# Weighted sums of an attention kernel: one TensorE run of four key blocks per four heads in place of two runs of two

## The chip, the cores and the metric

The kernel runs on one core of a Trainium2 chip. The metric is the device time of one execution in microseconds (us). The kernel before took 989.45 us, the median of 3 runs (988.32 to 992.9).

## What is computed

The reference is one adapter and one transformer block over `x` of 8 sequences, 512 tokens and 256 channels. What matters here is the attention, with 16 heads of 16 channels and a bias and a mask for each pair of tokens:

```
q, k, v = (x @ Wq + bq), (x @ Wk + bk), (x @ Wv + bv)          # split into 16 heads of 16
scores  = einsum('bhqd,bhkd->bhqk', q / sqrt(16), k) + attention_bias
scores  = where(src_mask, -inf, scores)
probs   = softmax(scores, axis=-1)
ctx     = einsum('bhqk,bhkd->bhqd', probs, v)                   # the weighted sums
x       = x + (ctx @ Wo + bo)
out     = x + gelu2(layernorm(x) @ W1 + b1) @ W2 + b2
```

Ahead of it stands an adapter (`gelu(x @ down) @ expert @ up`, residual, layer norm), and a second layer norm whose scale and shift come from a time step.

## The kernel before

**Tiling.** The 4096 rows are cut into 16 chunks of 256 queries (two chunks to a sequence). An iteration `i` of the main loop holds the attention of chunk `i`; the loop runs over `i` = 0 to 16, the last one only finishes. The norm and projections of chunks `i+1` and `i+2`, the output projection of chunk `i-1` and the feed-forward part of chunks `i-1` and `i-2` are spread over the same iteration.

**Slots.** An iteration has 32 slots, `t` = 0 to 31. A slot is one tile of scores: 128 queries of one head against all 512 keys. Such a tile goes through the engines in this way:

- SyncE loads the bias of a head (two tiles) into one of 8 buffers `bias_s`, once PE has turned the head that used the buffer before.
- POOL subtracts the mask (L490, once for a head).
- PE computes the scores, `score(t)` (L806), into one of two banks `sc`. It waits until DVE has finished tile `t-2`, by semaphore `smax`.
- DVE adds bias and takes the row maximum, `find_max(t)` (L1338), a custom instruction and a short read of its accumulator `mx` behind it, which counts `smax`.
- ACT takes the exponential, `soften(t)` (L952).
- Four slots later (`LAG`) PE transposes the tile, `turn(n)` with `n = t-4` (L813), four blocks of 128 by 128, into one of two banks `tp`. It waits for the exponential and until tile `n-2` has been moved out of the bank.
- ACT, or DVE for the tiles 8, 10, 11, 13, 15, 17, 20, 23, 24, 25 and 27 of an iteration, copies it into the buffer `pT`, `move(n)` (L958, L1345). On ACT, the move of a slot stands ahead of the exponential of that slot.

**The weighted sums.** Four heads (8 tiles) make a group `g`; `pT` has a buffer for each of two groups. When the 8 tiles of a group have been moved, PE multiplies them with the values, `weigh` (L772): for each of four key blocks `kt`, four matmuls, one per head, each of 128 by 32 weights. Their `tile_position` puts them side by side in the array's columns, and each writes 32 partitions of the bank `pv`. Two groups accumulate into one `pv`, which DVE then multiplies with the inverse sums (L1318).

**What sets the order.** Each engine runs its program in order. Where the extra work of an iteration stands is written by hand in tables such as `PE_AT`: the whole part is the slot; fraction .0 is ahead of the slot's score, .3 between its score and its turn, .6 behind its turn. The engines never look ahead: PE's order alone decides when a score and a turn are issued. In `PE_AT` before, a group's sum has two entries, so the run stands in two halves, one ahead of the score of slot 14 and one ahead of the score of slot 15 for the first group, 22 and 23 for the second, 30 and 31 for the third; the fourth stands in the next iteration, ahead of 6 and 7. This text calls them place 14, place 22, place 30 and place 6. The last group of all stands in iteration 16, where no score or turn is left between its two halves.

Of the kernel before, what the change touches and what calls it, by code (L numbers as in the profile page):

```python
# [25 lines left out]
NG = H // GH  # L26
TI = 2 * H
TG = 2 * GH
KT = S // P
# [13 lines left out]


PE_AT = dict(up=0.3, v=(1.0, 2.0), q=(8.6, 10.0), xt1=12.6, k=(15.6, 16.3), down=(24.3, 25.3),
             pv=((14.0, 15.0), (22.0, 23.0), (30.0, 31.0), (6.0, 7.0)), spread=(23.3, 7.3))
ACT_AT = dict(q=(11.0, 12.3), widen=(18.3, 2.3), spread=(24.6, 8.0), k=(17.0, 18.0), xT1=14.0, gelu=26.6)
DVE_AT = dict(x1=1.6, st0=2.3, mv0=2.6, v=3.0, n1=4.0, n2=6.3, st1=7.0, mv1=7.6, m1=8.3, m2=10.6, q=(11.6, 13.0),
              k=(17.6, 18.6), recip=(17.6, 1.6), ctx=(25.3, 9.3))
# [58 lines left out]
def wait(eng, sem, value):  # L108

    if value <= 0:  # L110
        return
    eng.wait_ge(sem, value)
# [7 lines left out]
def on_act(n):  # L120

    return n % TI not in DVE_MOVES


def moved(n, by_act):

    return sum(on_act(k) == by_act for k in range(n % TI)) + n // TI * (21 if by_act else 11)


def head_of(hh):  # L130

    return 8 * (hh // 8) + 2 * (hh % GH) + hh // GH % 2
# [17 lines left out]
def build(nc, x, x_t, t_tok, e_tok, bias, mask, downT, upT, up_b, experts, gamma, beta,  # L150
# [16 lines left out]
    with ExitStack() as ctx:  # L167
# [3 lines left out]
        def ps(name):  # L171
            return ctx.enter_context(nc.psum_tensor(name, [P, 512], F32))

        def sem(name):
            return ctx.enter_context(nc.semaphore(name))
# [86 lines left out]
        pv = ps("pv")  # L262
# [42 lines left out]
        s = {n: sem(n) for n in names}  # L305
# [246 lines left out]
        def _(pe):  # L552
# [63 lines left out]
            def fold_expert(b, bank, j):  # L616
                return pe.matmul(bank[0:A + 1, j * D:(j + 1) * D], ew_t[:, b, :], up_w, start=True, stop=True)
# [42 lines left out]
            for b in range(6, 8):  # L660
                last = fold_expert(b, tp[0], b % 2)
# [8 lines left out]
            def body(i, attn, prev, nxt, pre, qv, down):  # L670
                a, c = i + 2, i + 1
                AT = PE_AT

                def norm_steps(t):
                    if pre and t == AT["up"]:
                        wait(pe, s["a_xt1"], a)
                        wait(pe, s["d_out"], i - 2)
                        adapter_up(a)
                    if qv and t in AT["q"]:
                        if t == AT["q"][0]:  # L680
                            pe.wait_ge(s["d_v"], c + 1)
                        queries(c, AT["q"].index(t))
                    if qv and t in AT["v"]:
                        if t == AT["v"][0]:
                            pe.wait_ge(s["a_xt1"], c + 1)
                            pe.wait_ge(s["d_k"], c + 1)
                            wait(pe, s["a_hT"], i - 1)
                        values(c, AT["v"].index(t))
                    if pre and t in AT["k"]:
                        if t == AT["k"][0]:  # L690
                            pe.wait_ge(s["a_xt1"], a + 1)
                            pe.wait_ge(s["d_q"], c + 1)
                        keys(a, AT["k"].index(t))
                    if pre and t == AT["xt1"]:
                        turn_rows(a)
                    if down and t in AT["down"]:
                        if t == AT["down"][0]:
                            wait(pe, s["d_act"], 4 * (i - 1))
                        adapter_down((i + 3) // 2, AT["down"].index(t))
# [40 lines left out]
                def mid_steps(m, at):  # L740
                    when = mid_at(m)
                    if at in when["wo"]:
                        j = when["wo"].index(at)
                        if j == 0:
                            pe.wait_ge(s["d_ctx"], 2 * m + 2)
                            pe.wait_ge(s["d_k"], min(a + 1, NCH))
                            pe.wait_ge(s["d_q"], min(c + 1, NCH))
                            wait(pe, s["a_hT"], m)
                            if m >= NCH - 2:
                                pe.wait_ge(s["d_act"], 4 * (m - 1) + (2 if m == NCH - 2 else 4))  # L750
                        for ct in range(CT):
                            last = pe.matmul(lb[:, j * D:(j + 1) * D], ctxn[:, ct, j * P:(j + 1) * P],  # L752
                                             wo_s[:, ct, :], start=(ct == 0), stop=(ct == CT - 1))
                        if j == 1:
                            last.then_inc(s["p_wo"], 1)
                    if at == when["ht"]:
                        pe.wait_ge(s["d_hn"], m + 1)
                        transposes(lb, hn, "p_ht")

                def weigh(g, half):  # L760
                    gi = NG * i + g - (NG if g == NG - 1 else 0)
                    if half == 0:
                        pe.wait_ge(s["copied_v"], moved(TG * (gi + 1), False))
                        pe.wait_ge(s["copied_a"], moved(TG * (gi + 1), True))
                        pe.wait_ge(s["d_v"], 2 * (gi // NG // 2) + 2)
                        if g % 2 == 0:
                            wait(pe, s["d_ctx"], gi // 2)
                    v = v_all[(gi // NG // 2) % 2]
                    for kt in range(2 * half, 2 * half + 2):
                        for h in range(GH):  # L770
                            col = HD + 2 * HD * head_of(GH * g + h) - HD * (g % 2)
                            last = pe.matmul(pv[32 * h:32 * h + 32, 0:CH], v[:, kt, col:col + 2 * HD],  # L772
                                             pT[gi % 2][:, h, kt, :], start=(g % 2 == 0 and kt == 0),
                                             stop=(g % 2 == 1 and kt == KT - 1), tile_position=(0, 32 * h))
                    if half == 1:
                        last.then_inc(s["pv_done"], 1)

                def spread_inverses(r):
                    ri = 2 * (i - r) + r
                    pe.wait_ge(s["a_wide"], ri + 1)  # L780
                    wait(pe, s["a_rin"], ri)
                    for j in range(2):
                        last = pe.transpose(inverse_bank(ri)[:, CH + j * P:CH + (j + 1) * P],
                                            rwide[:, j, :], ident[:, :])
                    last.then_inc(s["p_rin"], 1)

                def steps(t, at):
                    norm_steps(t)
                    for f in range(max(0, i - 2), min(i, NCH)):
                        ffn_steps(f, at)  # L790
                    if i > 0:
                        mid_steps(i - 1, at)
                    for g in range(NG):
                        if (prev if g == NG - 1 else attn) and t in AT["pv"][g]:
                            weigh(g, AT["pv"][g].index(t))
                    for r in range(2):
                        if (prev if r else attn) and t == (4.0 if i == NCH else AT["spread"][r]):
                            spread_inverses(r)
# [25 lines left out]
                for t in range(TI):  # L824
                    each_slot(i, t, steps, lambda: score(t) if attn else None,
                              lambda: turn(TI * i + t - LAG) if (attn if t >= LAG else prev) else None)
# [590 lines left out]
```

## Time and profile before

| | |
|---|---|
| median of 3 runs | 989.45 us (988.32 to 992.9) |
| profiled execution, its own time | 990.3 us |
| its span, first to last instruction | 988.4 us |
| granted TensorE clock, mean | 0.969 of full speed |
| PE busy | 918.3 us, 93% |
| DVE, ACT, POOL busy | 715.2, 708.5, 685.4 us |
| share of the DMA queue's packets | 69.9% of 16 engines |

A busy engine is not yet the bound: what ends last at each wait is. Rows of a timeline give the start and the length of a merged piece of equal instructions. A matmul's length there runs to its modelled end, and the next matmul starts before that, so the pace of PE is read from start to start. The compiler makes two records of a float32 matmul, so 8 matmuls of `weigh` show as 16; the transposes show as one each. Iterations 2 to 14 take 54.6 and 56.9 us in turn.

### The profile page before, as it was taken

The numbers are of one execution on the slowest core, as the hardware profiler recorded it, in microseconds if no ns is written. First come the engines' busy times: TensorE is split into PE (matmuls) and PEld (weight loads), VectorE is DVE, ScalarE is ACT, GpSimd is POOL, SyncE is SP. The second block draws the span as 40 slices with busy tenths as digits, with TensorE's granted clock in tenths as the row PEclk, the third lists the DMA queues.
The fourth block names the chain that finished last, engine by engine and source line by source line (L and its number), as shares of the span: only waits on it lengthen the run. The fifth ranks groups of instructions, "written<-read, shape, count | busy, mean of one in ns | idle before, by whom it ended". The sixth has DMA issues, their size and how long they took to land.

```text
span 988.4 us, 20949 instructions
## 1 busy us (share of the span) xinstructions
PE 918.3 (93%) x6621; PEld 663.4 (67%) x6621; DVE 715.2 (72%) x1911; ACT 708.5 (72%) x1675; POOL 685.4 (69%) x391
## 2 busy tenths in 40 slices
PE   3576989899999999999999999999999999999977
PEld 1344566677777776777777776777677777676755
DVE  6846787678687886878687786878687787675541
ACT  2235888778697787878697787878697787877641
POOL 2427995978677876978677875978687876774600
PEclk8768999999999999999999999999999999999998
DMA  5299979866887679776887679776887669764200
GB/s 168 84 259 325 295 232 259 231 208 203 246 252 218 214 209 271 228 206 204 241 259 219 214 209 265 223 212 202 236 250 219 203 198 266 229 185 149 81 11 11
DMA packets 147950, 207.42 MB, mean 210 GB/s; under 512 B 14385, under 2 KB 62322, under 8 KB 147842
## 3 DMA queue, kind: packets, MB, share of 16 engines
q1 hardware_dynamic: 147842, 206.09, 69.9%
q8 instruction: 55, 0.90, 0.4%
q14 instruction: 53, 0.43, 0.1%
HBM read 185.05 MB, written 20.99 MB: 208 GB/s over the span
## 4 chain that ended last, share of the span: by engine, by line
PE 80%; issue 7%; POOL 6%; DVE 5%; ACT 1%; DMA 1%; SPq 0%; POOLq 0%; DVEq 0%; ACTq 0%
PE tp L813 19%; PE pv L772 12%; PE la L735 11%; PE sc L806 11%; PE lc L718 10%; POOL bias_s L490 5%; PE lb L582 4%; PE lb L752 3%; PE lb L598 2%; PE lc L716 1%; DVE xm L1089 1%; PE la L572 1%; PE lc L564 1%; PE la L556 1%; PE lb L556 1%
## 5 line engine op out<-in xcount | busy, mean ns | idle before, releaser
L490 POOL TENSOR_TENSOR bias_s<-mask_f,bias_s 128x1024 f32<-128x1024 f32 x256 | 603.1, 2373 | 188.4 <-DMA bias_s<-in_bias 188.1
L1338 DVE CUSTOM_DVE_ANT_0 bias_s<-sc,bias_s 128x512 f32<-128x512 f32 x512 | 349.2, 685 | 189.8 <-PE sc L806 179.2
L952 ACT ACTIVATE bias_s<-bias_s,mx 128x512 f32<-128x512 f32 x512 | 371.6, 726 | 107.4 <-DVE mx L1338 104.0
L813 PE MATMUL tp<-ident,bias_s 128*128 128x128 f32 x2048 | 311.7, 275 | 8.1 <-ACT pT L958 4.9
L813 PEld LDWEIGHTS tp<-ident,bias_s 128*128 128x128 f32 x2048 | 252.7, 142 | 89.7 <-issue 19.1
L958 ACT COPY pT<-tp 128x512 f32<-128x512 f32 x336 | 195.9, 583 | 101.9 <-PE tp L813 99.5
L806 PE MATMUL sc<-stk,stq 128*128 128x512 bf16 x512 | 197.7, 387 | 17.1 <-DVE mx L1338 15.0
L772 PE MATMUL pv<-pT,v_all 128*32 128x256 f32 x2048 | 137.3, 386 | 0.2 <-issue 0.2
L735 PE MATMUL la<-w_s,act_s 128*128 128x256 f32 x512 | 128.3, 380 | 0.2 <-DVE act_s L1297 0.2
L1345 DVE COPY pT<-tp 128x512 f32<-128x512 f32 x176 | 120.6, 685 | 4.6 <-PE tp L813 4.5
L718 PE MATMUL lc<-hT,w_s 128*128 128x256 f32 x464 | 121.1, 384 | 0.0
L806 PEld LDWEIGHTS sc<-stk,stq 128*128 128x128 bf16 x512 | 50.1, 98 | 81.6 <-DVE mx L1338 41.4
L952 ACT ACTIVATION_READ_ACCUMULATOR bias_s<-bias_s,mx 128x1 f32 x512 | 98.6, 193 | 0.0
L735 PEld LDWEIGHTS la<-w_s,act_s 128*128 128x128 f32 x512 | 89.2, 190 | 8.8 <-DVE act_s L1297 0.4
L718 PEld LDWEIGHTS lc<-hT,w_s 128*128 128x128 f32 x464 | 80.2, 193 | 10.8 <-issue 0.3
L772 PEld LDWEIGHTS pv<-pT,v_all 128*32 128x32 f32 x2048 | 53.9, 109 | 48.7 <-issue 26.2
L500 POOL TENSOR_SCALAR rs<-mv 128x2 f32<-128x2 f32 x48 | 9.3, 193 | 78.4 <-DVE mv L1084 76.0
L1297 DVE SCALAR_TENSOR_TENSOR act_s<-th,lc 128x512 f32<-128x512 f32 x57 | 38.9, 683 | 10.8 <-ACT th L918 10.8
L1338 DVE DVE_READ_ACCUMULATOR2_ANT mx<- 128x1 f32 x512 | 42.6, 83 | 0.0
L501 POOL TENSOR_TENSOR rs<-rs,powc 128x2 f32<-128x2 f32 x48 | 33.5, 699 | 4.0
L716 PE MATMUL lc<-b1sel,b1p 128*128 128x256 bf16 x116 | 31.9, 275 | 3.2 <-ACT hT L910 2.7
L752 PE MATMUL lb<-wo_s,ctxn 128*128 128x256 f32 x128 | 33.0, 381 | 1.4 <-DVE ctxn L1318 1.4
(188 smaller groups left out, 845.4 us busy)
## 6 DMA issues: line engine op xcount, KB each, us to landing
bias_s<-in_bias SPq DMA_DIRECT2D x256, 512.0 KB, 4.3
stq<-q_parts SPq DMA_DIRECT2D x128, 96.0 KB, 3.7
stk<-k_parts SPq DMA_DIRECT2D x128, 96.0 KB, 3.9
k_parts<-kb SPq DMA_DIRECT2D x32, 192.0 KB, 2.3
q_parts<-qb SPq DMA_DIRECT2D x32, 192.0 KB, 2.4
xT<-in_x_t SPq DMA_DIRECT2D x8, 512.0 KB, 5.6
k_parts<-kb SPq DMA_DIRECT2D x32, 128.0 KB, 2.3
stq<-q_parts SPq DMA_DIRECT2D x64, 64.0 KB, 3.8
```

The costliest lines, as they stand in the source:

```text
L490: pool.tensor_tensor(tile, mask_f[:, :, :], tile, ALU.subtract).then_inc(s["masked"], 1)
L716: pe.matmul(h, b1p[:, :], b1sel[:, ft:ft + 1].to_broadcast([P, CH]), start=True, stop=False)
L718: last = pe.matmul(h, w1_s[:, ct, ft * P:(ft + 1) * P], hT[:, ct, :], start=False, stop=(ct == CT - 1))
L735: last = pe.matmul(rows, act_s[:, ft, j * P:(j + 1) * P], w2_s[:, ft, :], start=False, stop=(ft == FT - 1))
L752: last = pe.matmul(lb[:, j * D:(j + 1) * D], ctxn[:, ct, j * P:(j + 1) * P], wo_s[:, ct, :], start=(ct == 0), stop=(ct == CT - 1))
L772: last = pe.matmul(pv[32 * h:32 * h + 32, 0:CH], v[:, kt, col:col + 2 * HD], pT[gi % 2][:, h, kt, :], start=(g % 2 == 0 and kt == 0), stop ...
L806: pe.matmul(sc[t % 2][:, :].rearrange("p (e k) -> p e k", e=2), stq[:, hh, j * P:(j + 1) * P], stk[:, :, hh, :], start=True, stop=True).th ...
L813: last = pe.transpose(tp[n % 2][:, kt * P:(kt + 1) * P], bias_s[:, n // 2 % NB, n % 2, kt * P:(kt + 1) * P], ident[:, :])
L952: act.activation(tile, tile, ACT.Exp, bias=mx[:, t:t + 1], scale=-1.0, accum_out=sums[:, j, head_of(hh):head_of(hh) + 1]).then_inc(s["prob ...
L958: act.copy(pT[n // TG % 2][:, n // 2 % GH, :, (n % 2) * P:(n % 2 + 1) * P], tp[n % 2][:, :].rearrange("p (k q) -> p k q", k=KT)).then_inc( ...
L1338: dve.tensor_tensor_reduce(out=tile, in0=sc[t % 2][:, :], in1=tile, scale=1.0, scalar=BIG, op0=ALU.add, op1=ALU.min, accum_out=mx[:, t:t + ...
L1345: dve.tensor_copy(pT[n // TG % 2][:, n // 2 % GH, :, (n % 2) * P:(n % 2 + 1) * P], tp[n % 2][:, :].rearrange("p (k q) -> p k q", k=KT)).th ...
```

## The change

`weigh` loses its second argument and its run covers all four key blocks. Its entry in `PE_AT` is one number for each group: 14.6, 22.6, 30.6 and 6.6, which is behind the turn of slot 14 and ahead of the score of slot 15. The number of matmuls, their operands, the waits ahead of the first and the count behind the last are the same; what changes is the order on PE. The orders of ACT, DVE, POOL and SyncE stay as they were (there, too, ACT's move stands ahead of its exponential, before and after).

```diff
-             pv=((14.0, 15.0), (22.0, 23.0), (30.0, 31.0), (6.0, 7.0)), spread=(23.3, 7.3))
+             pv=(14.6, 22.6, 30.6, 6.6), spread=(23.3, 7.3))
...
-                def weigh(g, half):
+                def weigh(g):
                     gi = NG * i + g - (NG if g == NG - 1 else 0)
-                    if half == 0:
-                        pe.wait_ge(s["copied_v"], moved(TG * (gi + 1), False))
-                        pe.wait_ge(s["copied_a"], moved(TG * (gi + 1), True))
-                        pe.wait_ge(s["d_v"], 2 * (gi // NG // 2) + 2)
-                        if g % 2 == 0:
-                            wait(pe, s["d_ctx"], gi // 2)
+                    pe.wait_ge(s["copied_v"], moved(TG * (gi + 1), False))
+                    pe.wait_ge(s["copied_a"], moved(TG * (gi + 1), True))
+                    pe.wait_ge(s["d_v"], 2 * (gi // NG // 2) + 2)
+                    if g % 2 == 0:
+                        wait(pe, s["d_ctx"], gi // 2)
                     v = v_all[(gi // NG // 2) % 2]
-                    for kt in range(2 * half, 2 * half + 2):
+                    for kt in range(KT):
...
-                    if half == 1:
-                        last.then_inc(s["pv_done"], 1)
+                    last.then_inc(s["pv_done"], 1)
...
-                        if (prev if g == NG - 1 else attn) and t in AT["pv"][g]:
-                            weigh(g, AT["pv"][g].index(t))
+                        if (prev if g == NG - 1 else attn) and t == AT["pv"][g]:
+                            weigh(g)
```

On PE at place 6, the slots 4 to 7 of an iteration, the order before (`sc` is a score, `tp` a turn, `pv<-pT,v_all` the weighted sum, `pv<-ident,rwide` the spreading of the inverse sums):

```order
L806 MATMUL sc<-stk,stq 128x512
L813 MATMUL tp<-ident,bias_s 128x128 x4
L806 MATMUL sc<-stk,stq 128x512
L813 MATMUL tp<-ident,bias_s 128x128 x4
L772 MATMUL pv<-pT,v_all 32x256 x8
L806 MATMUL sc<-stk,stq 128x512
L813 MATMUL tp<-ident,bias_s 128x128 x4
L772 MATMUL pv<-pT,v_all 32x256 x8
L806 MATMUL sc<-stk,stq 128x512
L783 MATMUL pv<-ident,rwide 128x128 x2
```

and the same place in the changed kernel:

```order
L804 MATMUL sc<-stk,stq 128x512
L811 MATMUL tp<-ident,bias_s 128x128 x4
L804 MATMUL sc<-stk,stq 128x512
L811 MATMUL tp<-ident,bias_s 128x128 x4
L804 MATMUL sc<-stk,stq 128x512
L811 MATMUL tp<-ident,bias_s 128x128 x4
L771 MATMUL pv<-pT,v_all 32x256 x16
L804 MATMUL sc<-stk,stq 128x512
L781 MATMUL pv<-ident,rwide 128x128 x2
```

The score and the turn of slot 6 now stand ahead of all of the weighted sum, so three scores and turns follow each other with nothing between. The score of slot 7 has the same work ahead of it as before.

On PE at place 30, from the transposes of the normed rows (`lb<-ident,hn`, between slots 28 and 29) to the first work of the next iteration, before:

```order
L556 MATMUL lb<-ident,hn 128x128 x4
L806 MATMUL sc<-stk,stq 128x512
L813 MATMUL tp<-ident,bias_s 128x128 x4
L772 MATMUL pv<-pT,v_all 32x256 x8
L806 MATMUL sc<-stk,stq 128x512
L813 MATMUL tp<-ident,bias_s 128x128 x4
L772 MATMUL pv<-pT,v_all 32x256 x8
L806 MATMUL sc<-stk,stq 128x512
```

and changed:

```order
L556 MATMUL lb<-ident,hn 128x128 x4
L804 MATMUL sc<-stk,stq 128x512
L811 MATMUL tp<-ident,bias_s 128x128 x4
L804 MATMUL sc<-stk,stq 128x512
L811 MATMUL tp<-ident,bias_s 128x128 x4
L771 MATMUL pv<-pT,v_all 32x256 x16
L804 MATMUL sc<-stk,stq 128x512
```

Here it is the score and the turn of slot 30 that move ahead of the first half. Places 14 and 22 change alike.

## Rows read from the trace of the kernel before

**Rows 1.** The page: busy time of PE, share of the span, instructions.

```profile
PE 918.3 (93%) x6621; PEld 663.4 (67%) x6621; DVE 715.2 (72%) x1911; ACT 708.5 (72%) x1675; POOL 685.4 (69%) x391
```

**Rows 2.** Windows view: stretch, busy us of each engine, PEclk, DMA share, GB/s.

```profile
187.00:851.00 664.00, 659.95 (x4931) 485.55 (x4930) 510.84 (x1363) 525.56 (x1248) 510.56 (x286) 1.00 0.76 225
```

**Rows 3.** Groups by line, POOL, 56 to 187 us: busy, mean ns, idle before, releaser.

```profile
L490 POOL TENSOR_TENSOR bias_s<-mask_f,bias_s 128x1024 f32<-128x1024 f32 x39 | 91.4, 2368 | 45.6 <-DMA bias_s<-in_bias 45.4
```

**Rows 4.** Timeline of PE at place 6, iteration 8: start us, length us, what.

```profile
508.71 0.60 PE L813 MATMUL tp<-ident,bias_s 128*128 128x128 f32 x4
509.15 0.38 PE L806 MATMUL sc<-stk,stq 128*128 128x512 bf16 x1
509.37 0.60 PE L813 MATMUL tp<-ident,bias_s 128*128 128x128 f32 x4
509.90 1.07 PE L772 MATMUL pv<-pT,v_all 128*32 128x256 f32 x16
510.90 0.39 PE L806 MATMUL sc<-stk,stq 128*128 128x512 bf16 x1
511.13 0.60 PE L813 MATMUL tp<-ident,bias_s 128*128 128x128 f32 x4
...
512.66 0.39 PE L806 MATMUL sc<-stk,stq 128*128 128x512 bf16 x1
```

**Rows 5.** Timeline of PE, iteration 16: both halves of the last group back to back.

```profile
955.79 1.93 PE L772 MATMUL pv<-pT,v_all 128*32 128x256 f32 x32 [0.21 <-issue]
```

**Rows 6.** Timelines of DVE and PE where PE waited for DVE, iteration 0.

```profile
95.77 0.69 DVE L1345 COPY pT<-tp 128x512 f32<-128x512 f32 x1
...
96.60 0.63 PE L813 MATMUL tp<-ident,bias_s 128*128 128x128 f32 x4 [0.23 <-DVE pT L1345]
...
98.37 0.09 DVE L1338 DVE_READ_ACCUMULATOR2_ANT mx<- 128x1 f32 x1
...
98.51 0.39 PE L806 MATMUL sc<-stk,stq 128*128 128x512 bf16 x1 [1.28 <-DVE mx L1338]
```

**Rows 7.** Timeline of DVE around place 6, iteration 8.

```profile
504.28 0.69 DVE L1338 CUSTOM_DVE_ANT_0 bias_s<-sc,bias_s 128x512 f32<-128x512 f32 x1 [1.13 <-PE sc L806]
...
510.02 0.08 DVE L1338 DVE_READ_ACCUMULATOR2_ANT mx<- 128x1 f32 x1
...
517.56 0.69 DVE L1338 CUSTOM_DVE_ANT_0 bias_s<-sc,bias_s 128x512 f32<-128x512 f32 x1 [1.00 <-PE sc L806]
```

**Rows 8.** Timelines of PE and DVE at place 6, iteration 14.

```profile
841.10 1.07 PE L772 MATMUL pv<-pT,v_all 128*32 128x256 f32 x16
...
841.22 0.08 DVE L1338 DVE_READ_ACCUMULATOR2_ANT mx<- 128x1 f32 x1
```

**Rows 9.** Timelines of DVE and PE at place 14, iteration 8.

```profile
523.08 0.69 DVE L1345 COPY pT<-tp 128x512 f32<-128x512 f32 x1
...
524.41 1.07 PE L772 MATMUL pv<-pT,v_all 128*32 128x256 f32 x16
```

**Rows 10.** Timelines of DVE and PE at place 22, iteration 8.

```profile
537.43 0.08 DVE L1338 DVE_READ_ACCUMULATOR2_ANT mx<- 128x1 f32 x1
...
539.10 1.07 PE L772 MATMUL pv<-pT,v_all 128*32 128x256 f32 x16
```

**Rows 11.** Timelines of DVE and PE at place 30, iteration 8.

```profile
551.83 0.69 DVE L1345 COPY pT<-tp 128x512 f32<-128x512 f32 x1
...
552.49 1.07 PE L772 MATMUL pv<-pT,v_all 128*32 128x256 f32 x16
```

**Rows 12.** Timelines of PE and DVE at place 14, iteration 1.

```profile
134.36 1.07 PE L772 MATMUL pv<-pT,v_all 128*32 128x256 f32 x16
...
134.62 0.69 DVE L1345 COPY pT<-tp 128x512 f32<-128x512 f32 x1
```

**Rows 13.** Timelines of DVE and PE at place 14, iteration 15.

```profile
911.86 0.67 DVE L1345 COPY pT<-tp 128x512 f32<-128x512 f32 x1
...
914.24 0.39 PE L806 MATMUL sc<-stk,stq 128*128 128x512 bf16 x1
```

## The prediction, made before the changed kernel had run

> **What bounds the kernel now.** First the page: PE is busy 93% of the span, the next engine 72% [rows 1]. That is an average, so the windows view comes second: from 187 to 851 us (iterations 2 to 14, two thirds of the span) PE is busy 659.95 of 664.00 us at a granted clock of 1.00, and DVE, ACT and POOL have about 140 us or more to spare in it [rows 2]. In that stretch whatever PE no longer has to do shortens the kernel, and whatever new wait PE gets lengthens it. In the first iterations it is otherwise: from 56 to 187 us POOL masks 39 heads in 91.4 us and sits idle 45.6 us for the bias transfers [rows 3], so POOL and the transfers set the pace and PE waits for what comes of them.
>
> Third, the timeline of PE at one place, to see what a half run costs from start to start. Two slots with nothing between them, turn to turn, take 509.37 - 508.71 = 0.66 us. With a half run between, turn to turn takes 511.13 - 509.37 = 1.76 us [rows 4]. The half thus costs 1.10 us. Its work is four steps (two records for each of two key blocks, four heads at a time). A step's own pace comes from the one place where both halves already follow each other: 32 records last 1.93 us there and 16 last 1.07 us, so four more steps cost 0.86 us, 0.215 us each [rows 4, 5]. Of the 1.10 us, 0.86 are work and 0.24 are the way into the 32-column form and out of it again. The parts agree: turn to weighted sum is 0.53 us and turn to score 0.44 (0.09 going in); weighted sum to score is 1.00 us where four steps make 0.86 (0.14 coming out, the slower first step included); the score after it leads by 0.23 instead of 0.22 (0.01) [rows 4]. I take 0.245 us for a way in and out, between the 0.24 of the one and the 0.25 that rounding allows.
>
> The Trainium skill (TensorEngine Tiling (Array Packing), Key Properties) says that a change of tiling mode, though not a change of tile, drains TensorE. The trace agrees in kind, with 0.24 us for a change there and back. Read alone, that page would promise the whole saving at every place (the second case below).
>
> **What the change takes away.** The last group already runs in one piece [rows 5], so 63 of 64 groups lose one way in and out: 63 x 0.245 = 15.4 us, if nothing else moved. No matmul, wait or semaphore count is added or removed, no DMA moves, and the other four engines keep their orders.
>
> **What it moves.** At each place one score and one turn (slots 14, 22, 30 and 6) are issued a half run, 1.10 us, sooner relative to the PE work around them. Everything behind the run has the same PE work ahead of it as before, less 0.245 us. So the only new waits can be those of these two instructions. The score waits until DVE has finished tile t-2; the turn waits until tile n-2 has left the bank. Where PE did wait for DVE, a score started 98.51 - (98.37 + 0.09) = 0.05 us after the maximum ended, and a turn 96.60 - (95.77 + 0.69) = 0.14 us after the copy ended [rows 6]. Now each place, the moved score taken at the start of the first half less the 0.09 us of the way in:
>
> Place 6. The score could start at 509.81. The maximum it needs ends at 510.02 + 0.08 = 510.10 [rows 7], so it starts at 510.15: a new wait of 0.35 us. DVE cannot be sooner: from 504.28, where it last waited for a score, it works through without a pause to beyond 510 [rows 7]. The turn follows it by 0.22, at 510.37, by which time its bank should be free: the tile two before it, turned at 508.71, is moved by ACT ahead of an exponential. The net at this place is -0.245 + 0.35 = +0.105 us. The whole stretch moves with PE: DVE waits for PE at 504.28 and again, by 1.00 us, at 517.56 [rows 7], so the 0.1 us is neither given back nor multiplied. Iteration 14 gives the same: ready at 841.10 - 0.09 = 841.01, needed maximum at 841.30, wait 0.34 [rows 8]. These two are the seventh and the last of 13 such places, iterations 2 to 14, with the same wait to 0.01 us; the first of them lies in the start.
>
> Place 14. Score ready at 524.32, turn 0.22 later at 524.54; the copy it needs ends at 523.77 and is usable at 523.91 [rows 9]. No wait: -0.245.
>
> Place 22. Score ready at 539.01, the maximum ends at 537.51 [rows 10]; the copy for the turn is as old. No wait: -0.245.
>
> Place 30. Score ready at 552.40, turn at 552.62; the copy ends at 552.52 and is usable at 552.66 [rows 11]. Wait 0.04: net -0.20. This is the narrowest place; 0.1 us more in the copy would go straight onto PE.
>
> An iteration in which PE sets the pace gains 0.245 + 0.245 + 0.20 - 0.105 = 0.585 us. The behaviour of DVE and ACT behind the run is not at risk by these rows: they get one tile sooner and the next at the same moment as before.
>
> **The sum.** Iterations 3 to 13: 11 x 0.585 = 6.4 us. Iteration 14: 0.6. Iteration 2 without its place 6, which still lies in the start: 0.245 + 0.245 + 0.20 = 0.7.
>
> Iteration 15: places 6, 22 and 30 have room and gain 0.245 each, 0.735 in all. At place 14 the copy ends late, at 911.86 + 0.67 = 912.53, so the turn cannot start before 912.67. The run of eight steps follows it by 0.53 and lasts 1.00 + 0.86 = 1.86 us to the next score, at 915.06 instead of 914.24 [rows 13, 4]: +0.82. Together +0.1.
>
> The start, the remaining 8 places: the lower bound is 8 x 0.245 = 2.0 us of gain. For the upper one I take iteration 1, place 14: the copy ends at 135.31, the turn starts at 135.45, the run at 135.98, the next score at 137.84; before it stood at 134.36 + 1.76 + 1.00 = 137.12 [rows 12, 4], so +0.7. Places like it there, each priced by the same arithmetic, add to at most 2.3 us. Most of it must vanish, because POOL and the bias transfers decide when these iterations end [rows 3]; but buffers come free by PE's turns, so not all. I take +0.3.
>
> Sum: -6.4 - 0.6 - 0.7 + 0.1 + 0.3 = -7.3 us. The profiled execution took 990.3 us, 1.9 above its span, and gives 983.0. It lies 0.85 us above the median of the runs; against 989.45 the forecast is 982.1 us, 0.7% less.
>
> **The rivals.**
>
> (1) The forecast, 982.1 us, its own range 980 to 984.5. Chance 0.60.
>
> (2) The waits at the moved scores cost nothing, and the whole 15.4 us come: 974.0 us. For it speaks that places 14 and 22 have room of 0.6 and 1.5 us and place 30 all but enough; against it that the maximum at place 6 is late by arithmetic on DVE's unbroken work [rows 7]. It is also what the page's rule gives by itself. Chance 0.10.
>
> (3) No change that can be measured. The gain is real, but place 30 waits like place 6, since its room is 0.1 us and less than the 0.14 us a copy needs to be seen [rows 6, 11]: another 0.3 us in 13 iterations, 3.9 us. With 2.3 instead of 0.3 us at the start this is -7.3 + 3.9 + 2.0 = -1.4, or 988.0 us. Chance 0.23.
>
> (4) Slower. The run in one piece keeps new scores and turns from DVE and ACT for 1.86 us where a half kept them for 1.00. If at one place of the iteration they cannot make up the 0.86 us before PE asks for the tile, PE waits it out: place 30 is the candidate, with only two bare slots around its run, 15 x 0.86 = 12.9 us, so 995 us. It decides once the waits added beyond those priced here pass 7.3 us, that is 0.12 us at each of 63 runs. Against it: DVE waits for a score, by 1.13 and 1.00 us, on both sides of place 6 [rows 7], so it has caught up each time. Chance 0.07.
>
> That the change does not do what it says is excluded by the order of the instructions.
>
> **How the numbers follow.** What a measurement of this kernel can tell from no change is about 0.5%, 5 us; so faster means below 984.5 and slower above 994.4. Faster takes cases 1 and 2 and a little of 3: 0.72. Same: 0.21. Slower: 0.07. The range reaches from 977, a forecast with half of place 6's waits gone (2.3 us) and the start at its lower bound (2.3 us), to 987, which takes in most of case 3. Left out are case 2, most of case 4 and the end of 3, about 2 in 10.
>
> **What would show it.** In the changed kernel's profile the weighted sum should show as 64 runs of 32 records of 1.93 us, with 1.86 us to the next score. The score ahead of place 6 should start 0.05 us behind DVE's maximum, 1.0 us behind the score before it instead of 0.65; iterations should be shorter by 0.6 us. The prediction is wrong if the way in and out is not saved (a run longer than 1.93 us), if the wait at place 6 is absent (iterations shorter by 0.9 us), or if PE waits for copies at place 30 or after the runs.

## The result, and the profile after

The changed kernel takes 983.96 us, the median of 8 runs (981.71 to 986.22); the kernel before took 989.70 us in its 8 runs (988.32 to 992.9). The ratio is 0.9937, 95% interval 0.9919 to 0.9956: 0.6% faster, 6.2 us by the ratio. The forecast was 982.1 us in a range of 977 to 987, 7.3 us less than before. The profiled execution took 984.5 us, its span 982.7.

First the page of the changed kernel, the line that answers to [rows 1]:

```profile
PE 904.6 (92%) x6621; PEld 670.7 (68%) x6621; DVE 714.3 (73%) x1911; ACT 708.9 (72%) x1675; POOL 685.5 (70%) x391
```

PE is busy 13.7 us less, but the profiled execution is only 5.8 us shorter (984.5 for 990.3): about 8 us of what PE no longer does has become waiting. The windows view of the same stretch as [rows 2], where PE was idle 4.05 us and now is 6.75:

```profile
187.00:851.00 664.00, 657.25 (x4974) 496.29 (x4978) 515.78 (x1377) 531.65 (x1263) 515.75 (x287) 1.00 0.76 227
```

Where a part of the waiting sits is seen at place 6 of iteration 8, which answers to [rows 4] and [rows 7]. The timeline of PE (start us, length us, what, idle before and releaser), then of DVE:

```profile
506.96 0.38 PE L804 MATMUL sc<-stk,stq 128*128 128x512 bf16 x1
507.17 0.60 PE L811 MATMUL tp<-ident,bias_s 128*128 128x128 f32 x4
507.96 0.39 PE L804 MATMUL sc<-stk,stq 128*128 128x512 bf16 x1 [0.19 <-DVE mx L1336]
508.19 0.60 PE L811 MATMUL tp<-ident,bias_s 128*128 128x128 f32 x4
508.72 1.93 PE L771 MATMUL pv<-pT,v_all 128*32 128x256 f32 x32
510.58 0.39 PE L804 MATMUL sc<-stk,stq 128*128 128x512 bf16 x1
```

```profile
507.82 0.08 DVE L1336 DVE_READ_ACCUMULATOR2_ANT mx<- 128x1 f32 x1
```

The score of slot 6 stands 1.00 us behind the one before it where two bare slots are 0.66 us apart, and starts 0.06 us after the maximum that it waits for has ended at 507.90. The view calls 0.19 us of that idle, because it counts from a matmul's modelled end; start to start the wait is 0.35 us. The run that follows is 32 records in 1.93 us and 1.86 us to the next score. All this is as forecast, to 0.01 us.

Place 30 of iteration 8 (to be read with [rows 11]), timelines of DVE and PE:

```profile
549.26 0.69 DVE L1343 COPY pT<-tp 128x512 f32<-128x512 f32 x1
...
549.83 0.38 PE L804 MATMUL sc<-stk,stq 128*128 128x512 bf16 x1
...
550.09 0.63 PE L811 MATMUL tp<-ident,bias_s 128*128 128x128 f32 x4
550.65 1.93 PE L771 MATMUL pv<-pT,v_all 128*32 128x256 f32 x32
```

The turn comes 0.26 us behind its score in place of 0.22, 0.14 us after the copy's end at 549.95, and is itself 0.03 us longer. The weight loads show why: its first one starts at 550.06, 0.03 us ahead of it, where a turn that does not wait has its first weights loaded earlier (before, at 509.15 for the turn at 509.37). That is 0.07 us in all, where 0.04 were forecast. And place 14 of iteration 15 (with [rows 13]):

```profile
905.70 0.68 DVE L1343 COPY pT<-tp 128x512 f32<-128x512 f32 x1
...
906.52 0.63 PE L811 MATMUL tp<-ident,bias_s 128*128 128x128 f32 x4 [0.96 <-DVE pT L1343]
907.08 1.93 PE L771 MATMUL pv<-pT,v_all 128*32 128x256 f32 x32
908.95 0.39 PE L804 MATMUL sc<-stk,stq 128*128 128x512 bf16 x1
```

The turn starts 0.14 us after the copy has ended at 906.38, and the next score 2.43 us behind the turn, where the forecast had 2.39. Counted from the score of slot 13, this score comes 0.86 us later than before; 0.82 were forecast.

How much an iteration changes is read from a score that stands at the same place of the order in both kernels, that of slot 8, in iterations 3 and 14. Timeline of PE, the kernel before:

```profile
234.71 0.38 PE L806 MATMUL sc<-stk,stq 128*128 128x512 bf16 x1
...
845.72 0.38 PE L806 MATMUL sc<-stk,stq 128*128 128x512 bf16 x1
```

and changed:

```profile
235.25 0.38 PE L804 MATMUL sc<-stk,stq 128*128 128x512 bf16 x1
...
840.44 0.38 PE L804 MATMUL sc<-stk,stq 128*128 128x512 bf16 x1
```

Eleven iterations take 605.19 in place of 611.01 us: 5.82 us less, 0.53 us each. (The 54.6 and 56.9 us in turn that were told of iterations 2 to 14 hold for 3 to 12; 2 takes 58.9, 13 takes 54.6 and 14 takes 52.4 us.) The same two scores are the measure of the experiments below, since the median of a whole kernel moves by a few us from run to run.

### The profile page after: what moved, and what is told of

Same layout as the page of the kernel before. It is cut to its first block, busy times and chain, and to the rows that moved or that the text cites. A ratio compares the mean times of both kernels' runs of the same rounds, so it can differ in the third digit from the quotient of the medians.

```text
span 982.7 us, 20949 instructions
## 1 busy us (share of the span) xinstructions
PE 904.6 (92%) x6621; PEld 670.7 (68%) x6621; DVE 714.3 (73%) x1911; ACT 708.9 (72%) x1675; POOL 685.5 (70%) x391
## 4 chain that ended last, share of the span: by engine, by line
PE 67%; issue 12%; POOL 9%; DVE 9%; DMA 2%; ACT 1%; DVEq 0%; POOLq 0%; SPq 0%; ACTq 0%
PE tp L811 15%; PE pv L771 10%; PE la L735 10%; PE sc L804 9%; PE lc L718 8%; POOL bias_s L490 8%; PE lb L582 4%; PE lb L752 3%; DVE bias_s L1336 2%; DMA bias_s<-in_bias 1%; DVE la L1087 1%; DVE st L1075 1%; PE lc L716 1%; DVE xm L1087 1%; PE lb L598 1%
## 5 line engine op out<-in xcount | busy, mean ns | idle before, releaser
L735 PE MATMUL la<-w_s,act_s 128*128 128x256 f32 x512 | 128.3, 380 | 0.2 <-DVE act_s L1295 0.2
L771 PE MATMUL pv<-pT,v_all 128*32 128x256 f32 x2048 | 123.8, 382 | 0.2 <-issue 0.2
L735 PEld LDWEIGHTS la<-w_s,act_s 128*128 128x128 f32 x512 | 89.2, 190 | 8.9 <-DVE act_s L1295 0.4
L771 PEld LDWEIGHTS pv<-pT,v_all 128*32 128x32 f32 x2048 | 60.2, 109 | 43.8 <-issue 10.9
L752 PE MATMUL lb<-wo_s,ctxn 128*128 128x256 f32 x128 | 33.0, 381 | 1.4 <-DVE ctxn L1316 1.4
```

The costliest lines, as they stand in the source:

```text
L735: last = pe.matmul(rows, act_s[:, ft, j * P:(j + 1) * P], w2_s[:, ft, :], start=False, stop=(ft == FT - 1))
```

## The experiments

Every experiment was timed beside the kernel before on its chip. "Per iteration" is the difference from before between the scores of slot 8 in iterations 3 and 14, divided by 11.

**e1: all runs one score and one turn earlier.**

```diff
-             pv=(14.6, 22.6, 30.6, 6.6), spread=(23.3, 7.3))
+             pv=(14.0, 22.0, 30.0, 6.0), spread=(23.3, 7.3))
```

> The changed kernel with its run of four key blocks one score and one turn earlier: ahead of the scores of slots 14, 22, 30 and 6 in place of behind their turns. Theory A (a way into and out of the 32-column form costs 0.24 us, and what the change lost again are PE's waits at the score and the turn that it moved ahead of the run): those two are behind the run now, so the waits at place 6 (0.35 us), at place 30 (0.07 us) and at place 14 of iterations 1 and 15 (0.7 and 0.86 us over the gain) go, and each iteration from 2 to 14 is 0.96 us shorter than before in place of 0.53. The time is 11 to 15 us under that of before, 975 to 979 us. Rival B (the run in one piece is worth 0.13 us a place because DVE and ACT starve for 1.86 us, wherever it stands): 983 to 985 us, as the change.

981.19 us (978.98 to 983.29, 6 runs), ratio 0.9911 (0.9892 to 0.9930). Per iteration -0.85 us (601.67 for 611.01) instead of -0.53: most of the way to A's 0.96, and against B. The median lies between the two expectations, 2 us above A's, and the interval overlaps the change's own, so it is the trace that decides against B. The step at which A was short in each iteration is place 30. Timeline of PE there:

```profile
549.32 0.38 PE L804 MATMUL sc<-stk,stq 128*128 128x512 bf16 x1
549.54 0.60 PE L811 MATMUL tp<-ident,bias_s 128*128 128x128 f32 x4
550.07 0.38 PE L804 MATMUL sc<-stk,stq 128*128 128x512 bf16 x1
```

Now it is the score of slot 0, three bare slots behind the run, that comes 0.53 us behind the turn ahead of it instead of 0.44, and 0.15 us after DVE's maximum of slot 30 has ended at 549.92, in each of these iterations: moving the run forward only moves the close scores and turns behind it, and at this place they then outrun DVE by 0.1 us. Iterations 14 and 15 lose more behind runs that now stand earlier: 0.55 us at slots 16 and 17 of iteration 14, 0.44 and 0.38 at slots 0 and 24 of iteration 15.

**e2: place 6 alone ahead of the score.**

```diff
-             pv=(14.6, 22.6, 30.6, 6.6), spread=(23.3, 7.3))
+             pv=(14.6, 22.6, 30.6, 6.0), spread=(23.3, 7.3))
```

> The changed kernel with the run of the fourth group alone ahead of the score of slot 6, the other three behind their turns as changed. Theory A: the wait of 0.35 us at place 6 goes in iterations 2 to 14 and nothing else changes, so 4 to 5 us less than the changed kernel, 979 to 980 us, and 0.88 us per iteration under before. Rival B (starving, wherever the run stands): no difference from the changed kernel, 984 us.

979.32 us (977.99 to 981.5, 5 runs), ratio 0.9892 (0.9872 to 0.9911); per iteration -0.89 us. Both of A's numbers, and the interval lies below the change's own; by the ratios it is 4.5 us less. Timeline of PE at place 6:

```profile
504.70 0.38 PE L804 MATMUL sc<-stk,stq 128*128 128x512 bf16 x1
...
505.45 1.93 PE L771 MATMUL pv<-pT,v_all 128*32 128x256 f32 x32
507.32 0.39 PE L804 MATMUL sc<-stk,stq 128*128 128x512 bf16 x1
```

The run has taken the place of the wait: nothing here is idle.

**e3: the move without the merge** (the kernel before, its halves kept).

```diff
-             pv=((14.0, 15.0), (22.0, 23.0), (30.0, 31.0), (6.0, 7.0)), spread=(23.3, 7.3))
+             pv=((14.6, 15.3), (22.6, 23.3), (30.6, 31.3), (6.6, 7.3)), spread=(23.3, 7.3))
```

> The kernel before with the two halves kept apart but moved behind the turn of slot 14 and behind the score of slot 15 (22 and 23, 30 and 31, 6 and 7 alike). The score and the turn of slots 14, 22, 30 and 6 come as early as in the change, and no way into or out of the 32-column form is saved. Theory A: the waits at the moved scores come without the saving: 0.35 and 0.04 to 0.07 us more per iteration in 13 iterations, 5 us, about 1 us in iteration 15 and up to 2 at the start, so 994 to 998 us. Rival C (where the score stands is free, and the change gains 0.13 us a place from another cause): 990 us.

998.59 us (997.99 to 999.47, 4 runs), ratio 1.0083 (1.0062 to 1.0104); per iteration +0.61 us (617.72 for 611.01). Where the score stands is not free: C falls. The time is 0.6 us over A's upper end, and per iteration A had 0.39 to 0.42. Timeline of PE at place 6:

```profile
514.72 0.38 PE L806 MATMUL sc<-stk,stq 128*128 128x512 bf16 x1
...
515.73 0.39 PE L806 MATMUL sc<-stk,stq 128*128 128x512 bf16 x1 [0.19 <-DVE mx L1338]
...
517.49 0.39 PE L806 MATMUL sc<-stk,stq 128*128 128x512 bf16 x1
517.81 1.07 PE L772 MATMUL pv<-pT,v_all 128*32 128x256 f32 x16
518.81 0.44 PE L783 MATMUL pv<-ident,rwide 128*128 128x128 f32 x2
```

The score is again 1.01 us behind the one before it, the same wait. What A missed is 0.04 to 0.06 us a place: the half that is left into transposes costs more than the one left into a score (the two transposes behind it last 0.44 us where they elsewhere last 0.38). The same 0.05 us a place stand in e4 and e6.

**e4: four runs of one key block** (the kernel before, `weigh` with `kt` = its second argument).

```diff
-             pv=((14.0, 15.0), (22.0, 23.0), (30.0, 31.0), (6.0, 7.0)), spread=(23.3, 7.3))
+             pv=((14.0, 14.3, 15.0, 15.3), (22.0, 22.3, 23.0, 23.3), (30.0, 30.3, 31.0, 31.3), (6.0, 6.3, 7.0, 7.3)), spread=(23.3, 7.3))
...
-                    for kt in range(2 * half, 2 * half + 2):
+                    for kt in range(half, half + 1):
...
-                    if half == 1:
+                    if half == 3:
```

> The kernel before with each sum in four runs of one key block: ahead of the score of a slot and between its score and its turn, and the same in the next slot. It adds two ways into and out of the 32-column form to each of 63 groups and no work. Theory A (0.24 us a way in and out): 126 x 0.24 = 30 us more, 1018 to 1022 us. Rival D (the 0.24 us are not the change of form but the first matmuls waiting for the moved tiles or for the bank pv, and come once a group): 990 to 992 us.

1022.52 us (1021.53 to 1023.62, 4 runs), ratio 1.0331 (1.0309 to 1.0353), 32 us more, 0.5 us over A's range; per iteration +2.30 us (636.29 for 611.01) for eight more ways in and out, 0.29 us each. The eight that were added all stand between a score and a turn. D falls. Timeline of PE at place 6:

```profile
524.14 0.64 PE L772 MATMUL pv<-pT,v_all 128*32 128x256 f32 x8
524.71 0.39 PE L806 MATMUL sc<-stk,stq 128*128 128x512 bf16 x1
525.03 0.64 PE L772 MATMUL pv<-pT,v_all 128*32 128x256 f32 x8
525.60 0.66 PE L813 MATMUL tp<-ident,bias_s 128*128 128x128 f32 x4
526.19 0.64 PE L772 MATMUL pv<-pT,v_all 128*32 128x256 f32 x8
```

Two steps take 0.57 us where their work is 0.43, every time, also for the second, third and fourth quarter, which wait for nothing new. A turn between two runs lasts 0.59 us from start to start where turn to weighted sum was 0.53 [rows 4]; this is the 0.05 us that a way out into transposes costs over one into a score.

**e5: each run at its better place.**

```diff
-             pv=(14.6, 22.6, 30.6, 6.6), spread=(23.3, 7.3))
+             pv=(14.0, 22.0, 30.6, 6.0), spread=(23.3, 7.3))
```

> The changed kernel with each run where the waits priced so far are least: ahead of the scores of slots 14, 22 and 6, behind the turn of slot 30. Theory A: per iteration 0.24 + 0.24 + 0.17 + 0.24 = 0.89 us under before, as with place 6 alone moved back; on top the 0.86 us at place 14 of iteration 15 and 0.7 to 1.4 us at place 14 of iterations 0 and 1 come back, because the late copy now has the run to hide under. So 1.5 to 2.5 us less than the kernel with place 6 alone moved back, 977 to 978 us. Rival B (the places do not matter beyond place 6): 979.3 us, as that kernel.

980.38 us (979.57 to 981.89, 5 runs), ratio 0.9900 (0.9879 to 0.9921); per iteration -0.89 us. The trace shows the late copy of iteration 15 hidden, the score straight behind the run at 905.03 and no wait ahead of it, but the time is 2.4 us over A's range and not below e2's. Why is said at e9.

**e6: between score and turn.**

```diff
-             pv=(14.6, 22.6, 30.6, 6.6), spread=(23.3, 7.3))
+             pv=(14.3, 22.3, 30.3, 6.3), spread=(23.3, 7.3))
```

> The changed kernel with all runs between the score and the turn of slots 14, 22, 30 and 6: the score still comes ahead of the run, the turn no longer does. Theory A: place 6 waits for the maximum, at the score, so its 0.35 us stay; the waits at the turn go (0.07 us at place 30; at place 14 of iteration 15 a gain of 0.24 in place of a loss of 0.86). Per iteration 0.61 us under before, in all 1 us of steady iterations, 1.1 of iteration 15 and about 1 of the start under the changed kernel: 980 to 982 us. Rival E (it is the turn, or the bank that it needs, that waits at place 6): the wait of place 6 goes too, 976 to 978 us.

984.63 us (980.95 to 985.21, 6 runs), ratio 0.9928 (0.9906 to 0.9949); per iteration -0.40 us (606.57 for 611.01) where A had -0.61. The time is 2.6 us above A's range. Timeline of PE at place 6:

```profile
507.70 0.38 PE L804 MATMUL sc<-stk,stq 128*128 128x512 bf16 x1
...
508.70 0.39 PE L804 MATMUL sc<-stk,stq 128*128 128x512 bf16 x1 [0.19 <-DVE mx L1336]
509.02 1.93 PE L771 MATMUL pv<-pT,v_all 128*32 128x256 f32 x32
510.89 0.66 PE L811 MATMUL tp<-ident,bias_s 128*128 128x128 f32 x4
```

The wait is at the score, 1.00 us behind the one before, with the turn out of its way: E falls. A's number is short because its price of a way in and out, 0.24 us, is that of one between a turn and a score; the one used here, between a score and a turn, costs the 0.29 us of e4. Four places at 0.05 us are the 0.2 us per iteration that are missing, and 2.6 us in 13 iterations.

**e7: the maximum sooner on DVE**, PE's order as changed.

```diff
-DVE_AT = dict(x1=1.6, st0=2.3, mv0=2.6, v=3.0, n1=4.0, n2=6.3, st1=7.0, mv1=7.6, m1=8.3, m2=10.6, q=(11.6, 13.0),
+DVE_AT = dict(x1=1.6, st0=2.3, mv0=2.6, v=3.0, n1=4.6, n2=6.3, st1=7.0, mv1=7.6, m1=8.3, m2=10.6, q=(11.6, 13.0),
```

> The changed kernel, PE's order untouched; on DVE the centring of the rows (0.88 us) moves from ahead of to behind the maximum of slot 4. Theory A: the score at place 6 waits for that maximum alone, which now ends 0.4 us or more sooner, so the wait of 0.35 us goes in iterations 2 to 14: 4 to 5 us under the changed kernel, 979 to 980 us. Rival F (the wait at place 6 comes of DVE and ACT starving during a run in one piece, or of the DMA pace, and only shows at this score): no change, 984 us.

981.02 us (980.55 to 985.53, 6 runs), ratio 0.9917 (0.9894 to 0.9939). The times alone do not part it from the changed kernel beside it (e8), whose interval overlaps; the trace does: per iteration -0.68 us (603.53 for 611.01), 0.15 us of the 0.35 that A expected. Timelines at place 6, PE and ACT:

```profile
504.85 0.38 PE L804 MATMUL sc<-stk,stq 128*128 128x512 bf16 x1
...
505.16 0.56 ACT L956 COPY pT<-tp 128x512 f32<-128x512 f32 x1
...
505.51 0.39 PE L804 MATMUL sc<-stk,stq 128*128 128x512 bf16 x1
...
505.87 0.63 PE L811 MATMUL tp<-ident,bias_s 128*128 128x128 f32 x4
506.43 1.93 PE L771 MATMUL pv<-pT,v_all 128*32 128x256 f32 x32
```

The score is back at 0.66 us behind the one before it, so its wait was for the maximum and F falls. But the turn behind it now comes 0.36 us after its score instead of 0.22: it waits for ACT's copy of tile 0, which ends at 505.72, and becomes usable 0.15 us later. That wait was there all along, behind the longer one: in the changed kernel the same copy ends at 507.83, 0.15 us later is 507.98, and without the score's wait the turn would have stood at 507.84.

**e8: the changed kernel again.**

> The changed kernel once more, on the same chip and in the same rounds as the three others, as their base: 983 to 985 us by either theory. Its start differs from run to run; a second profile shows whether the 0.6 us by which the first 81 us were late in the first one belong to the change (then they come again) or to the run (then they need not).

984.59 us (983.45 to 985.89, 6 runs), ratio 0.9937 (0.9918 to 0.9955): the first result once more. Eleven iterations take 605.17 us (from 236.52 to 841.69), 0.02 us from the first profile. The first score of the loop starts at 59.91 in this profile, at 58.28 in the first and at 58.55 before, although nothing of the change lies ahead of it: that is a difference between executions. From this score to that of slot 10 of iteration 0, still ahead of the first merged run, it takes 25.32 us before, 26.16 in the first profile and 25.07 in this one. The 0.6 us did not come again, so they do not belong to the change.

**e9 and e10: e5 and e2 side by side**, with no further edit.

> The kernel with mixed places once more, beside the one with place 6 alone moved back, on one chip in the same rounds. In the traces the mixed one gains 1.6 us over the other from slot 8 of iteration 14 to the end (1.74 against 0.17 us under before), by the late copy at place 14 of iteration 15; theory A: it is 1 to 2 us the faster of the two, 978 to 980 us. Rival: the difference drowns in what the start differs from run to run (the first score of the loop stood between 0.3 us earlier and 1.4 us later than before in the profiles so far): the two agree to 1 us.

> The kernel with place 6 alone moved back once more, as base for the mixed one: 979 to 981 us.

e9: 979.12 us (977.8 to 980.95, 5 runs), ratio 0.9900 (0.9885 to 0.9916). e10: 980.32 us (977.9 to 982.07, 5 runs), ratio 0.9911 (0.9896 to 0.9926). Per iteration -0.89 and -0.82 us; the second holds one wait of 0.77 us for a copy of ACT, at slot 12 of iteration 8, which the first profile of that kernel does not have. This time the mixed one is 1.2 us the lower, in the first pair it was 1.1 us the higher.

The traces show why A's 1 to 2 us do not come. From slot 8 of iteration 14 to the last score of the loop the mixed kernel takes 104.30 us in both profiles, the other one 104.54 and 104.53. Place 14 of iteration 15 does give 1.2 us, but 0.9 of them go again in waits behind the runs that now stand earlier: 0.55 us at slots 16 and 17 of iteration 14, where a turn waits for a copy of DVE, and 0.38 at slot 24 of iteration 15. Most of the 1.6 us that the expectation for e9 took from the first pair lay behind the last score, where the order is the same in both: 38.02 us at a mean granted clock of 0.87 in e2 against 36.67 us at 0.91 in e5. The same kernel as e2 takes 36.55 us at 0.91 there in e10. So 0.2 us are left of the gain, too few for these runs to show. By the ratios the four results are 9 to 11 us under the kernel before and 2.6 to 4.5 us under the changed one (the intervals of e2 and e9 lie below its own, those of e5 and e10 reach into it); which of the two is better stays open.

## Why the prediction was right

**The way in and out, 0.24 to 0.245 us: shown.** Doubling the number of runs (e4) costs 0.29 us for each way added, taking one away (places 14 and 22) gives 0.24. One rival was not tested by a run: that any run of matmuls between a turn and a score costs as much, whatever its form. The kernel before settles it. Between the turn of slot 9 and the score of slot 10 of iteration 8 it has a run of four steps over the whole array. Timeline of PE:

```profile
517.23 0.60 PE L813 MATMUL tp<-ident,bias_s 128*128 128x128 f32 x4
517.66 1.03 PE L582 MATMUL lb<-xT,wq_s 128*128 128x256 f32 x4
518.53 0.38 PE L806 MATMUL sc<-stk,stq 128*128 128x512 bf16 x1
```

The score stands 1.30 us behind the turn, which is the bare 0.44 and the 0.86 of four steps, and nothing besides. The half run of [rows 4], the same four steps in the 32-column form, makes it 1.53. In iterations 3 to 13 a run of four such steps over the whole array stands 110 times between a turn and a score, from four lines of the kernel (L582, L598, L735, L752): 105 of them cost 0.86 or 0.87 us, five 0.91 or 0.92. It is the form that costs.

The Trainium skill's rule that a change of tiling mode drains TensorE (TensorEngine Tiling (Array Packing), Key Properties) agrees in kind with e4; the rule says nothing of what stands on either side, which here makes 0.05 us.

**The wait at place 6, 0.35 us, for DVE's maximum of slot 4: shown** from three sides. It comes without the merge (e3), it goes when the run stands ahead of the score (e2: per iteration 0.36 us less than the change, 4.5 us in time), and it leaves the score when DVE finishes the maximum sooner (e7). One sentence of the prediction was too easy: that the turn behind it finds its bank free. It did, but only because the score came 0.35 us late; without that, 0.17 us come at the turn (0.14 of wait, 0.03 in its slower first transpose), as e7 shows.

**The sum, piece by piece**, from the rows of the scores and in the first profile of the changed kernel. The eleven iterations: -5.82 us, forecast -6.4; at 0.53 instead of 0.585 us each. By place, as the mean of these iterations: 14 and 22 gain 0.24 each (forecast 0.245), 30 gains 0.17 (0.20), 6 loses 0.12 (0.105), and 0.01 go elsewhere. The term that was too small is the wait at place 30, 0.07 us for 0.04, because the slower first transpose of a turn that waits was left out: sizes, not mechanisms. From slot 8 of iteration 14 to slot 8 of iteration 15: 55.17 for 56.04 us, -0.87, forecast -0.93. From there to the end: +0.38, forecast +0.33 (0.82 to be lost at place 14, where 0.86 were, and two gains of 0.245). So the late part was right to 0.1 us.

**The start** was where the guess stood, +0.3 us with -2.0 and +2.3 as bounds. Timeline of PE: the scores of slot 10 in iteration 0, ahead of the first merged run, and of slot 16 in iteration 2; before, in the changed kernel, and in its second profile:

```profile
83.87 0.63 PE L806 MATMUL sc<-stk,stq 128*128 128x512 bf16 x1
...
194.32 0.38 PE L806 MATMUL sc<-stk,stq 128*128 128x512 bf16 x1
```

```profile
84.44 0.63 PE L804 MATMUL sc<-stk,stq 128*128 128x512 bf16 x1
...
195.16 0.38 PE L804 MATMUL sc<-stk,stq 128*128 128x512 bf16 x1
```

```profile
84.98 0.63 PE L804 MATMUL sc<-stk,stq 128*128 128x512 bf16 x1
...
196.43 0.38 PE L804 MATMUL sc<-stk,stq 128*128 128x512 bf16 x1
```

110.45 us before, 110.72 and 111.45 changed: +0.3 and +1.0 us, where the forecast has +0.1 for this stretch (the +0.3 and one gain of place 14). Ahead of it, where no run has been merged, the first changed profile lost 0.6 us against before, 84.44 for 83.87. In the second it is 1.1 us behind before, but there the first score of the loop already comes 1.4 us late (e8). The mean granted clock from 84 to 195 us is 0.98 before, 0.97 and 0.94 in the two changed profiles. So two executions of the same kernel differ here by as much as the forecast and the result do. The first profile is 5.8 us under before where the forecast has 7.3; of these 1.5 us, 0.6 lie in the eleven iterations, 0.6 ahead of the first merged run, 0.2 in the start behind it and 0.1 in the late part. That the median came no further from the forecast is in part luck, since the guess for the start could have been off by 2 us with the same mechanism. How much of the start's loss belongs to the change was not settled: the local losses at place 14 were seen (in iteration 1 the score stands 0.96 us behind the turn ahead of it in place of 0.44, and its own turn 0.69 us behind the score in place of 0.22), but POOL and the transfers decide how much of them lasts.

**The rivals.** (2), waits that cost nothing: falls with e2 and e3. (3), a second wait as large at place 30: it was 0.07 us, and the start lost 0.3 and 1.0 us where this case had 2.3. (4), DVE and ACT starving for 1.86 us: falls with e2, in which three runs stand unchanged and the fourth is as long, and 0.24 us are gained at each place but 30, which gains 0.17.

## What to carry to other kernels

When two runs of column-tiled matmuls are merged, count the ways into and out of the form from start to start, and then look at what is pulled ahead of the merged run: here one score that the old order had covered with half a run cost 0.35 of the 0.96 us. The remedy was on the same line, the merged run at the place of the first half instead of the second, at that one place. A moved instruction's slack is read from the trace before, with what the wait itself adds (here 0.06 us behind a maximum, in e1 once 0.15, and 0.14 behind a copy); and where a wait is removed, the next instruction's slack is read as well, since it may have been hidden behind it.

## What the runs showed of the hardware that was not expected

The way in and out of the 32-column form depends on its neighbours: 0.24 us between a turn and a score, 0.29 us between a score and a turn (e4: eight of them, 2.30 us), in both cases at a granted clock of 1.00. A narrow run of another kind in the kernel before costs the same: the down projection (L564, weights of 128 by 64, two records of 512 columns) starts at 487.04 between a score at 486.73 and a turn at 488.04, and the next matmul follows at 488.53. Score to turn is 1.31 us in place of 0.22 and turn to next 0.49 in place of 0.44, 1.14 us in all. By an estimate that counts 512 columns as two steps of 0.215 us [rows 5], 0.28 us are left for the way.

The timeline of the weight loads of the kernel before shows what the way in and out looks like, at the half run of [rows 4] and at the run over the whole array above:

```profile
509.89 0.59 PEld L772 LDWEIGHTS pv<-pT,v_all 128*32 128x32 f32 x16 [0.17 <-issue]
510.89 0.10 PEld L806 LDWEIGHTS sc<-stk,stq 128*128 128x128 bf16 x1 [0.41 <-DVE mx L1338]
...
517.55 0.73 PEld L582 LDWEIGHTS lb<-xT,wq_s 128*128 128x128 f32 x4
518.31 0.10 PEld L806 LDWEIGHTS sc<-stk,stq 128*128 128x128 bf16 x1
```

Going into the 32-column form, and coming out of it, the next weights are loaded 0.01 us ahead of their own matmul (at 509.90 and 510.90). Within the full form they are loaded 0.11 and 0.22 us ahead (matmuls at 517.66 and 518.53), under the work before. That the late load is all of the 0.24 us is not shown.

And a wait shows in the profile's idle column with only 0.19 of its 0.35 us, since idle time counts from the matmul's modelled end. That is why the idle time of PE from 187 to 851 us grew by only 2.7 us.
